# Macaron block on one core: the routed low-rank step as one pass of 98 rows

## The reference, cut to what matters

```python
y = jnp.einsum('bth,oh->bto', x, W_base) + b_base
A = lora_A[active]; Bm = lora_B[active]            # 4 experts, rank 8
z = jnp.einsum('bth,erh->bter', x, A)
contribs = jnp.einsum('bter,eor->bteo', z, Bm) * SCALING
alpha = jax.nn.softmax(jnp.log(prior + EPS) + logits, axis=-1)
return y + jnp.einsum('bteo,bte->bto', contribs, alpha)
```

## Time and profile before

| | us |
|---|---|
| median of 3 runs | 1154.39 |
| lowest and highest of them | 1153.88, 1154.97 |
| the profiled execution, its time | 1154.12 |
| the profiled execution, its span | 1152.3 |

### The profile page before, as it was taken

How to read it: one execution, slowest core, us unless ns; L and a number is a source line. 1 busy time by engine, 2 the same in 40 slices (tenths; PEclk the granted TensorE clock), 3 DMA queues, 4 the chain that set the end, 5 groups by cost and what they waited for, 6 DMA issues and landing times.

```text
span 1152.3 us, 21616 instructions
## 1 busy us (share of the span) xinstructions
PE 1092.8 (95%) x7156; PEld 891.4 (77%) x7156; DVE 908.4 (79%) x2667; ACT 607.0 (53%) x1738; POOL 705.5 (61%) x951
## 2 busy tenths in 40 slices
PE   5897999999998999999999899999999899999997
PEld 4755788888797788888788677888878678888876
DVE  4767888888676888888776888888867788888855
ACT  3554655555454655555534555555545455555542
POOL 2406877777432977777621887777723487777741
PEclk9998999999999999999999999999999999999998
DMA  9660000000101000000101000000010100000000
GB/s 285 186 195 1 1 1 1 1 1 1 38 10 65 1 1 1 1 1 1 37 1 38 37 1 1 1 1 1 1 38 28 47 2 1 2 1 2 1 2 36
DMA packets 22247, 30.94 MB, mean 27 GB/s; under 512 B 9302, under 2 KB 11094, under 8 KB 21498
## 3 DMA queue, kind: packets, MB, share of 16 engines
q1 hardware_dynamic: 19770, 24.85, 6.8%
q10 hardware_dynamic: 2368, 4.72, 1.2%
HBM read 22.23 MB, written 4.19 MB: 23 GB/s over the span
## 4 chain that ended last, share of the span: by engine, by line
PE 82%; DVE 9%; ACT 4%; issue 2%; POOL 1%; SPq 1%; DMA 1%; DVEq 0%; POOLq 0%
PE Y L992 15%; PE Y L966 13%; PE XZ L951 12%; PE Y L912 11%; PE XZ L930 6%; PE XZ L931 5%; PE XZ L932 5%; PE Y L681 4%; PE XZ L926 2%; PE XZ L681 2%; PE XZ L656 2%; DVE xT_lo L1297 1%; ACT xT_hi L1046 1%; DVE XZ L1638 1%; DVE q_turned L1580 1%
## 5 line engine op out<-in xcount | busy, mean ns | idle before, releaser
L1244 ACT ACTIVATE prob<-XZ,small 128x512 f32<-128x512 f32 (+3 forms) x512 | 266.7, 526 | 289.8 <-DVE small L1638 288.1
L637 POOL TENSOR_TENSOR prob<-prob,small 128x512 f32<-128x512 f32 (+3 forms) x512 | 361.0, 722 | 62.9 <-DVE small L1592 52.7
L1638 DVE CUSTOM_DVE_ANT_0 XZ<-XZ,mask 128x512 f32<-128x512 f32 (+3 forms) x512 | 248.0, 506 | 101.5 <-PE XZ L932 96.5
L542 POOL TENSOR_TENSOR q_sums<-q_sums,q_turned 64x512 f32<-64x512 f32 (+2 forms) x130 | 164.0, 1262 | 218.7 <-DVE q_turned L1580 217.2
L951 PE MATMUL XZ<-ident,prob 128*128 128x128 f32 x1280 | 196.0, 276 | 2.4 <-POOL prob L637 2.3
L951 PEld LDWEIGHTS XZ<-ident,prob 128*128 128x128 f32 x1280 | 150.4, 140 | 41.3 <-issue 10.3
L930 PE MATMUL XZ<-kT_hi,qT_hi 128*128 128x512 f32 (+2 forms) x384 | 148.0, 385 | 12.8 <-ACT prob L1244 9.1
L966 PE MATMUL Y<-probT,ckv 128*64 128x384 f32 (+2 forms) x1280 | 152.3, 384 | 0.0
L391 ACT ACTIVATE probT<-XZ 128x512 f32<-128x512 f32 x192 | 114.8, 598 | 64.9 <-PE XZ L951 63.9
L548 POOL TENSOR_TENSOR qT_lo<-q_sums,qT_hi 128x384 fp32r<-128x384 f32 (+2 forms) x130 | 130.1, 1001 | 23.2 <-ACT qT_hi L1211 22.7
L966 PEld LDWEIGHTS Y<-probT,ckv 128*64 128x64 f32 x1280 | 81.8, 136 | 64.2 <-issue 47.2
(11 more groups left out here) (225 smaller groups left out, 2219.7 us busy)
## 6 DMA issues: line engine op xcount, KB each, us to landing
wout_nat<-in_L_attn_w_out_dram SPq DMA_DIRECT2D x16, 512.0 KB, 4.6
out_dram<-x_sb SPq DMA_DIRECT2D x16, 256.0 KB, 2.0
x_next<-_attn_hidden_states_dram SPq DMA_DIRECT2D x12, 256.0 KB, 3.2
x_sb<-x_next SPq DMA_DIRECT2D x12, 256.0 KB, 2.3
wbase_nat<-in_L_ffn_W_base_dram ACTq DMA_DIRECT2D x1, 1024.0 KB, 5.7
x_sb<-_attn_hidden_states_dram ACTq DMA_DIRECT2D x4, 256.0 KB, 7.0
nope_a<-_L_attn_w_q_up_nope_dram ACTq DMA_DIRECT2D x1, 1024.0 KB, 5.5
rope_a<-_L_attn_w_q_up_rope_dram SPq DMA_DIRECT2D x1, 1024.0 KB, 8.0
```

Of the source, the lines that this page charges most:

```text
L542: nc.gpsimd.tensor_tensor(q, q, turned, ALU.add).then_inc(q_sum_set, 1)
L637: last = nc.gpsimd.tensor_tensor(prob[u % RING][:, c:c + w], prob[u % RING][:, c:c + w], inv_sum[:, u % RING, m:m + 1].broadcast_to([P, w] ...
L1244: last = nc.scalar.activation(prob[u % RING][:, c:c + w], score_ps[u % 2][:, c:c + w], ACT.Exp, bias=neg_max[:, u % RING, m:m + 1], scale= ...
L1638: last = nc.vector.tensor_tensor_reduce(bank, bank, mask[:, S - w:S], -1.0, HIGHEST, ALU.add, ALU.min, neg_max[:, u % RING, m:m + 1])
```

## The change

The gated values stand three times side by side in za (columns 0 to 31, 32 to 63, 64 to 95), followed by a column of 1, a column of -1 and zeros. The transposed tile goes into one tile zT: ScalarE writes high parts into all partitions, and z_low then overwrites partitions 64 to 95 with the low part. The weights lora_up hold high in partitions 0 to 31, low in 32 to 63 and high again in 64 to 95. Partition 96 holds the low part of the bias and partition 97 minus its high part, which the -1 turns back. One pass of 2 matmuls over 98 used rows gives the same three products and the bias. Addresses of the tiles placed behind za (down, k_sin) move by 1024 bytes, since two tiles fewer are placed.

```diff
@@ tiles
-        za = [place(f"za{i}", [P, 2, 64], F32, rb) for i in range(2)]
-        zT_hi = [place(f"zT_hi{i}", [P, P], F32R, rb) for i in range(2)]
-        zT_lo = [place(f"zT_lo{i}", [P, P], F32R, rb) for i in range(2)]
+        za = [place(f"za{i}", [P, P], F32, rb) for i in range(2)]
+        zT = [place(f"zT{i}", [P, P], F32R, rb) for i in range(2)]
@@ POOL: z_constants (ZB = 3 * NZ = 96)
-                        pad = ident[:, 0:2 * (63 - NZ)].rearrange("p (a z) -> p a z", a=2)
-                        nc.gpsimd.tensor_tensor(za[i][:, :, NZ + 1:64], pad, pad, ALU.subtract)
-                        nc.gpsimd.tensor_tensor(za[i][:, :, NZ], ones, ones, ALU.mult)
-                        last = nc.gpsimd.tensor_tensor(zT_lo[i][:], ident[:], ident[:], ALU.subtract)
+                        pad = ident[:, 0:P - ZB - 2]
+                        nc.gpsimd.tensor_tensor(za[i][:, ZB + 2:P], pad, pad, ALU.subtract)
+                        nc.gpsimd.tensor_tensor(za[i][:, ZB:ZB + 1], ones[:, 0:1], ones[:, 0:1], ALU.mult)
+                        last = nc.gpsimd.tensor_tensor(za[i][:, ZB + 1:ZB + 2], ones[:, 0:1], minus_one, ALU.mult)
@@ TensorE: lora
-                    for j, zt in enumerate((zT_hi, zT_lo)):
-                        for half in range(2):
-                            last = nc.tensor.matmul(banks_of(b, s)[:, half, 0:OH], zt[ffn_of(b, s) % 2][:],
-                                                    lora_up[:, half * OH:(half + 1) * OH],
-                                                    start=False, stop=(j == 1), skip_group_check=True)
+                    for half in range(2):
+                        last = nc.tensor.matmul(banks_of(b, s)[:, half, 0:OH], zT[ffn_of(b, s) % 2][:],
+                                                lora_up[:, half * OH:(half + 1) * OH],
+                                                start=False, stop=True, skip_group_check=True)
@@ ScalarE: z_high
-                    nc.scalar.activation(zT_hi[ffn_of(b, s) % 2][:], Z[0][:, 0:P], ACT.Copy).then_inc(zT_hi_set, 1)
+                    nc.scalar.activation(zT[ffn_of(b, s) % 2][:], Z[0][:, 0:P], ACT.Copy).then_inc(zT_hi_set, 1)
@@ VectorE: gate_rows
-                    for half in range(2):
-                        last = nc.vector.tensor_tensor(za[nth % 2][:, half, 0:NZ].rearrange("p (e r) -> p e r", e=NE),
-                                                       bank[:, 0, OH:OH + NZ].rearrange("p (e r) -> p e r", e=NE),
-                                                       gate, ALU.mult)
+                    z = bank[:, 0, OH:OH + NZ].rearrange("p (e r) -> p e r", e=NE)
+                    for k in range(3):
+                        last = nc.vector.tensor_tensor(za[nth % 2][:, k * NZ:(k + 1) * NZ]
+                                                       .rearrange("p (e r) -> p e r", e=NE), z, gate, ALU.mult)
@@ VectorE: z_low
-                    nc.vector.tensor_tensor(zT_lo[par][0:64, :], Z[0][0:64, 0:P], f32(zT_hi[par][0:64, :]),
+                    low = slice(2 * NZ, ZB)
+                    nc.vector.tensor_tensor(zT[par][low, :], Z[0][low, 0:P], f32(zT[par][low, :]),
                                             ALU.subtract).then_inc(zT_lo_set, 1)
@@ VectorE: fill_up
-                    for j in range(2):
-                        nc.vector.tensor_copy(up_nat[:, :, 64 * j:64 * j + NZ], up_b[:].rearrange("p c e r -> p c (e r)"))
-                        last = nc.vector.tensor_copy(up_nat[:, :, 64 * j + NZ:64 * j + NZ + 1], bias_nat[:].unsqueeze(2))
+                    for j in range(3):
+                        nc.vector.tensor_copy(up_nat[:, :, NZ * j:NZ * (j + 1)], up_b[:].rearrange("p c e r -> p c (e r)"))
+                    for j in range(2):
+                        last = nc.vector.tensor_copy(up_nat[:, :, ZB + j:ZB + j + 1], bias_nat[:].unsqueeze(2))
@@ VectorE: opening
-                    nc.vector.tensor_tensor(lora_up[64:P, :], weights_ps[0][64:P, :], f32(lora_up[64:P, :]),
-                                            ALU.subtract).then_inc(up_lo, 1)
+                    nc.vector.tensor_tensor(lora_up[NZ:2 * NZ, :], weights_ps[0][NZ:2 * NZ, :],
+                                            f32(lora_up[NZ:2 * NZ, :]), ALU.subtract)
+                    nc.vector.scalar_tensor_tensor(out=lora_up[ZB:P, :], in0=weights_ps[0][ZB:P, :],
+                                                   scalar=ident[ZB:P, ZB:ZB + 1], in1=f32(lora_up[ZB:P, :]),
+                                                   op0=ALU.mult, op1=ALU.subtract).then_inc(up_lo, 1)
```

More of the change, by code:

```diff
@@ L44 @@
 NZ = NE * R
+ZB = 3 * NZ
 EPS_LN = 1e-5
@@ L696, in transpose_z @@
                     pe.wait_ge(za_set, ffn_tile_of(b, s) + 1)
-                    nc.tensor.transpose(Z[0][:, 0:P], za[ffn_of(b, s) % 2][:].rearrange("p a z -> p (a z)"),
+                    nc.tensor.transpose(Z[0][:, 0:P], za[ffn_of(b, s) % 2][:],
                                         ident[:]).then_inc(zT_ps, 1)
@@ L1071, in ckT_high @@
                     if s == DOWN:
-                        home = za[0][:].rearrange("p a z -> p (a z)") if b < 0 else kT_top[:]
+                        home = za[0][:] if b < 0 else kT_top[:]
                         nc.scalar.activation(home, bank[:, 2 * P:3 * P], ACT.Copy, scale=SCORE_SCALE)
@@ L1106, in opening_queries @@
                     act.wait_ge(outw_ps, PAIRS)
-                    nc.scalar.activation(kT_top[:], za[0][:].rearrange("p a z -> p (a z)"), ACT.Copy)
+                    nc.scalar.activation(kT_top[:], za[0][:], ACT.Copy)
                     ckT_high(-1, STEPS - 1)
```

## The result

| | before | after |
|---|---|---|
| median, us | 1154.52 (8 runs, 1153.76 to 1155.29) | 1157.45 (8 runs, 1156.67 to 1159.99) |
| the profiled execution, its time | 1154.12 | 1157.63 |
| its span | 1152.3 | 1155.8 |

The changed kernel takes 1.0029 times as long (95% interval 1.0018 to 1.004), 2.9 us more. The forecast was 1155.3 us and "same" with 0.84; the result is slower by more than 0.2% and lies above the range, which ended at 1157.0.

The account below looks back on a forecast made before the run. Waits between TensorE and VectorE, not TensorE's 95% busy time, were taken to bound the kernel. Opening +0.07, mixed stages +1.87 and last stage -0.83 gave +1.1 us, forecast 1155.3 us, range 1152.7 to 1157.0.

Parts of the forecast that it names:

- Bounds and order of the work: Mixed stages: neither TensorE nor VectorE saturated; waits decide, and one of eight removed matmul pairs per stage counts.
- M: TensorE's queue: removing one of a tile's two low-rank matmul pairs takes -0.235 us per tile.
- A: VectorE: the third multiply of a tile costs +0.10 us, bounds 0.10 to 0.19.
- The walk through the tiles: Mixed stage: VectorE's lateness followed tile by tile, +0.86 by tile 0, only tile 2's pair paying, +0.62 us a stage.
- H: VectorE: z_low's changed start partition costs +0.10 us ahead of it and again behind it, bounds 0 to 0.12.
- the rival without a hold: VectorE at z_low: the changed start partition costs nothing, total -1.05, 1153.1 us; chance 0.22.
- lora_up and fill_up at nothing: Opening: an extra copy and a second instruction for the low weights cost 0, covered by waiting for the gate row.
- Last stage: Last feed-forward stage: TensorE leads, so removed pairs pay; -0.83 us together.
- the third rival, the clock: Mixed stages: TensorE's clock falls to half at a stage's end, 1.7 us or more each, 1160.3 us; chance 0.04.

Follow-up runs that it names:

- pair_out: The kernel before without its second low-rank pass (low x high product left out, 2 of 4 matmuls per tile), VectorE untouched: 1154.64 us, ratio 1.0002.
- after_two_passes: The changed kernel with its low-rank pass done twice, so TensorE has 4 matmuls per tile again: 1158.99 us, ratio 1.0042.
- old_high_start: The kernel before with z_low on partitions 64 to 127 instead of 0 to 63, nothing else changed: 1157.64 us, ratio 1.0025.
- low_first: The changed kernel with z_low on partitions 0 to 31 instead of 64 to 95: 1155.15 us, ratio 1.0004.
- before_all_filled: The kernel before with unread filler matmuls at the mixed stages' ends, in the opening and ahead of the last stage: 1152.07 us, ratio 0.9976.
- after_all_filled: The changed kernel with unread filler matmuls at the mixed stages' ends, in the opening and ahead of the last stage: 1155.76 us, ratio 1.0008.
- one_multiply: The changed kernel with a tile's three multiplies as one instruction over 96 columns, z_low still at partition 64: 1156.46 us, ratio 1.0009.
- after_filled: The changed kernel with five unread matmuls in TensorE's wait for the last update of each mixed stage: 1156.06 us, ratio 1.0015.
- both_all_filled: The changed kernel with z_low on partitions 0 to 31, one 96-column multiply, and fillers in all places: 1151.71 us, ratio 0.9966.
- both: The changed kernel with z_low on partitions 0 to 31 and the three multiplies as one of 96 columns: 1153.58 us, ratio 0.9985.
- before_filled: The kernel before with five unread matmuls in TensorE's wait for the last update of each mixed stage: 1153.86 us, ratio 0.9995.

## Why the prediction was wrong

**Bounds and order of the work: right.** Most of the removed pairs lie ahead of waits that VectorE ends. pair_out is the cleanest proof: 64 matmuls fewer, 7.5 us by their spacing, 0.4 us of each 270-us period.

**M: right as a term, too small as a gain.** The pair is 0.24 us of queue, and the one that counts is tile 2's, but 0.35 (after_two_passes) to 0.40 us (pair_out) a stage arrive. In pair_out 0.13 of that is there by tile 0, where the removed pairs take up part of the idle time of the earlier trace rows, and 0.27 come behind it. In the changed kernel that idle time is gone with the pair and without it, and what the 0.35 holds beyond the pair stays open.

**A: right as a term.** 0.10 us for an instruction more; by itself 0.17 to 0.30 us a stage, as VectorE is late from tile 5 on.

**The walk through the tiles: right in its order, with one slip.** At tile 0 the forecast's own terms make 0.70 + 0.30 - 0.16 = 0.84, not 0.76; 0.89 was measured. Without the slip the stage would have been forecast at +0.70.

**H: right, its upper bound.** 0.10 was forecast, 0.12 measured on each side, and old_high_start shows that the start partition alone does it. The rule of the Trainium skill ("VectorE: DVE Perf Modes", section on two Vector instructions with no wait between them) holds here for instructions as short as 0.29 us; the rival without a hold (0.22) is refuted by low_first, whose only difference is the start partition and whose period is 0.81 us shorter. A + H came to 0.93 against 0.86 (0.94 without the slip), M to -0.35 against -0.24, and +0.58 against the +0.62 of the forecast is luck in part: the slip of 0.08 and the larger M cancel most of each other.

**lora_up and fill_up at nothing: right.** The second instruction on lora_up (L1452, 20.49 us, 0.76 us long) ends 2.7 us ahead of the first logits.

**Last stage: too good.** -0.48 instead of -0.83. Both profiles have a half-clock stretch there, which neither starts nor ends at the same instruction in the two; at full clock throughout (before_all_filled and after_all_filled) the stage takes 19.91 us in the kernel before and 19.32 in the changed one, -0.59. Why 0.24 of the forecast's term is missing stays open.

**The step that failed: the third rival, the clock.** The forecast gave it 0.04, and argued from the whole stage: "the stage is 50.7 of 55 us busy, and would be some 48.8 of 55.6". That row is an average, and it hides the end of the stage, where TensorE was already busy only 1.5 of 3.40 us. The point from which the rival decides was named (a queue "as empty as ahead of 95 us") but never looked up. The forecast's row for it, 2.37 of 3.40 us, lies inside the half-clock stretch, which began at 93.4 us; ahead of it the kernel before shows

```profile
89.90:93.30 3.40, 1.13 (x10) 1.16 (x10) 2.44 (x8) 0.59 (x2) 2.53 (x3) 1.00 0.00 0
```

and the end of the changed kernel's mixed stages, with about 1.2, is nearly as empty. In the changed kernel's profile two of the three mixed stages were followed by a fall, 0.89 and 0.84 us, 1.73 of the 3.5 us between the profiles. Without them the profiled execution would have taken 1155.9 us, inside the range. And it differs from run to run: 57 of 79 runs of the kernel before had a mean clock of 0.993 or more, but 2 of 8 of the changed one.

**Its price.** The forecast's 1.7 us a fall is about twice what the two falls near 640 and 913 us cost. But it is less than the price of the falls that began inside an attention, behind a late landing of the rows: against the same stretch without one they cost 2.07 us (low_first, second period less first), 2.30 (one_multiply, the same) and 2.05 (after_all_filled). Such a landing alone, at full clock, cost 0.64 (pair_out).

**What decides whether the clock falls is not shown.** The change lengthens the hole at the mixed stage's end from 1.24 to 1.48 us, and a shorter TensorE queue alone does so too (1.50 us in pair_out). Filling it removed the falls. But a longer hole is neither enough nor needed: in pair_out's profile all three holes of 1.50 us, with TensorE busy about 1.2 of 3.40 us, passed at full clock, and old_high_start, whose hole is 1.24 us as before, has a fall behind the third and a mean clock of 0.992 or less in every run.

**What of the 2.9 us is shown.** The kernel before and the changed one, both filled, are 0.5 us under and 1.8 us over the unfilled kernel of their sets, 2.3 us apart; so the falls that these fillers remove account for about 0.6 of the 2.9. The forecast's own terms as measured make 0.06 + 1.74 - 0.48 = 1.3. The remaining 1.0 us is not attributed. It is not in the mean clock, which was 0.993 to 0.995 in all runs of both filled kernels, and it is not in their two profiles, whose spans differ by 1.3 us (1153.4 and 1152.1): the profile of after_filled is one of its faster runs (its time is 1155.23, the median 1156.06). A late landing of the rows would be such a cost, of 0.64 us in pair_out; whether it made the other runs slower, no trace tells.

## What to carry to other kernels

A split that puts a short VectorE operation on another group of partitions pays for it twice per use where VectorE has no gap; if the parts can be permuted, put the one that VectorE touches at partition 0 (0.81 us a stage here), and let one instruction write all copies (0.44). When a change makes TensorE's queue shorter or a hole in it longer, look up the emptiest few microseconds of each stage, not the stage's mean, and compare the two kernels at the same place in the work, not at the same time. Matmuls removed from a queue with holes may buy nothing. A hole that ends in dense work can be filled with matmuls that nobody reads; they cost nothing here, where they ended before the wait did (period 270.60 us with them, 270.58 without).

## What was not expected of the hardware

The clock's falls move. With the holes in the opening and ahead of the last stage filled, the kernel before ran at 0.999 or 1.0 throughout, 2.3 us faster; the profiled run of the changed kernel, with the same fillers, lost 2.05 us to a late landing and a fall that began at 919.2 us (and both_all_filled, at 916.8), where none of the profiles without fillers has one beginning. In low_first and one_multiply the fall of the second attention began at 648.7 and 650.4 us, not at 640.

These four have one thing in common. In each the copy of the next rows landed 4.1 to 4.4 us after its issue instead of 2.3, VectorE waited 0.63 to 0.92 us for it, TensorE's wait for the scores grew from 0.8 to between 1.55 and 1.83 us, and the fall began in that wait or within 0.7 us of its end. In pair_out the same wait, 1.54 us, was followed by none. In the changed kernel and in *both* the rows landed as late in the second attention (4.1 us), but a fall had come before, and VectorE did not wait. What made the landings late, the rows do not tell; the last copy of a mixed stage took 2.3 us in every stage of the profiles of before, before_filled, before_all_filled and old_high_start. One multiply over 96 columns takes 0.26 us and 0.17 us of queue, less than two over 32 columns (0.20).
